# Moving the operands of a split-product stage to common byte residues in SBUF

## The reference

```python
x = x + tanh(g_xattn[0]) * L0_xattn(layernorm(x), ctx, ctx, W, b)       # single-head attention, 154 keys
x = x + tanh(g_ffn[0])   * L0_ffn(layernorm(x), Wg, Wu, Wd)             # 8 dense experts, all summed
x = x + tanh(g_xattn[1]) * L1_xattn(layernorm(x), ctx, mask, gamma, beta, Wq, Wkv, Wout)  # 8 heads
x = x + tanh(g_ffn[1])   * L1_ffn(layernorm(x), wg, W, b)               # top-1 routing, capacity 256
# L0_ffn, per expert: acc += (silu(x @ wg) * (x @ wu)) @ wd     wg, wu: 256 x 1024, wd: 1024 x 256
```

## The kernel before, in words

| operands of the split products | role | before: start byte | mod 2048 | mod 512 |
|---|---|---|---|---|
| xop_hi, xop_lo (blocks at steps of 2,048) | moving | 116,064 to 171,360 | 1376 | 352 |
| hid_hi, hid_lo (blocks at steps of 2,048) | moving | 65,792 to 96,512 | 256 | 256 |
| t_hi, t_lo | moving | 20,608 to 30,848 | 128 | 128 |
| w_hi, w_lo (blocks at steps of 512) | stationary | 173,408 to 205,664 | 4 values | 352 |
| wd_hi, wd_lo (blocks at steps of 512) | stationary | 187,744 to 209,760 | 4 values | 352 |
| wds_hi, wds_lo | stationary | 16,512 to 20,096 | 4 values | 128 |

## Time and profile before

### The profile page before, as it was taken

The page is one execution under the profiler, slowest core; times in us unless marked ns, Lnnn a source line. Parts: engine busy times, 40 slices in busy tenths (PEclk is TensorE's granted clock), DMA queues, the critical chain, the costliest instruction groups (busy, mean ns, idle before and its releaser), DMA issues.

```text
span 1258.8 us, 18431 instructions
## 1 busy us (share of the span) xinstructions
PE 1232.6 (98%) x6152; PEld 995.4 (79%) x6152; DVE 1054.3 (84%) x1775; ACT 729.2 (58%) x1509; POOL 880.5 (70%) x833
## 2 busy tenths in 40 slices
PE   7999999999999999999999999999999999999998
PEld 5778888888888888888888888888888887787775
DVE  5887889898899999999999999888999974667546
ACT  2455566656666666666666666666566545545543
POOL 3735688888887888888877888888888626443435
PEclk9999999999999999999999999999999999999999
DMA  4020200000110000000000000000100330000131
GB/s 137 26 92 1 94 26 26 26 26 26 41 36 26 26 26 26 26 26 26 26 26 26 26 26 26 26 26 31 42 29 1 117 118 1 18 26 10 35 98 63
DMA packets 42366, 48.28 MB, mean 38 GB/s; under 512 B 4239, under 2 KB 40143, under 8 KB 42015
## 3 DMA queue, kind: packets, MB, share of 16 engines
q1 hardware_dynamic: 38720, 43.07, 10.4%
q0 software_dynamic: 1440, 3.41, 0.8%
q10 hardware_dynamic: 2111, 0.63, 0.2%
HBM read 37.36 MB, written 10.29 MB: 38 GB/s over the span
## 4 chain that ended last, share of the span: by engine, by line
PE 91%; DVE 4%; ACT 3%; issue 1%; DMA 0%; POOLq 0%; ACTq 0%; POOL 0%; DVEq 0%
PE bank L1307 25%; PE bank L1308 25%; PE bank L1309 25%; ACT PC L1050 2%; PE bank L1545 2%; PE bank L1554 1%; PE bank L1269 1%; PE bank L1707 1%; PE bank L1724 1%; PE bank L1251 1%; DVE nmC L2101 1%; PE bank L1529 1%; PE bank L1213 1%; PE bank L1657 1%; PE bank L1479 1%
## 5 line engine op out<-in xcount | busy, mean ns | idle before, releaser
L1307 PE MATMUL bank<-xop_hi,w_hi 128*128 128x512 f32 x896 | 351.9, 393 | 1.7 <-ACT half_g L948 1.2
L1308 PE MATMUL bank<-xop_lo,w_hi 128*128 128x512 f32 x896 | 352.4, 393 | 0.0
L1309 PE MATMUL bank<-xop_hi,w_lo 128*128 128x512 f32 x896 | 351.4, 392 | 0.0
L1958 DVE TENSOR_TENSOR hid_lo<-hid,hid_hi 128x512 fp32r<-128x512 f32 x228 | 220.2, 979 | 14.1 <-ACT hid_hi L972 9.8
L1307 PEld LDWEIGHTS bank<-xop_hi,w_hi 128*128 128x128 f32 x896 | 168.9, 188 | 42.4 <-ACT half_g L948 1.5
L1308 PEld LDWEIGHTS bank<-xop_lo,w_hi 128*128 128x128 f32 x896 | 168.6, 188 | 38.2
L1309 PEld LDWEIGHTS bank<-xop_hi,w_lo 128*128 128x128 f32 x896 | 168.6, 188 | 37.7
L972 ACT CAST hid_hi<-hid 128x512 fp32r<-128x512 f32 x228 | 140.8, 622 | 57.9 <-DVE hid L1950 57.9
L956 ACT ACTIVATE s<-bank 128x512 f32<-128x512 f32 x128 | 78.3, 612 | 102.5 <-PE bank L1309 102.5
L1307 PE MATMUL bank<-hid_hi,wd_hi 128*128 128x512 f32 x344 | 136.2, 396 | 0.6 <-DVE hid_lo L1958 0.6
L1308 PE MATMUL bank<-hid_lo,wd_hi 128*128 128x512 f32 x344 | 136.2, 396 | 0.0
(11 more groups left out here) (273 smaller groups left out, 2615.1 us busy)
## 6 DMA issues: line engine op xcount, KB each, us to landing
raw_gu<-in_L_ffn_Wg_dram SPq DMA_DIRECT2D x32, 256.0 KB, 2.7
raw_gu<-in_L_ffn_Wu_dram SPq DMA_DIRECT2D x32, 256.0 KB, 3.1
raw_d<-in_L_ffn_Wd_dram SPq DMA_DIRECT2D x32, 256.0 KB, 3.7
slots<-empty_row SPq DMA_DIRECT2D x1, 2080.0 KB, 11.1
xr<-slots SPq DMA_DIRECT2D x8, 260.0 KB, 4.5
x_res<-in_x_dram SPq DMA_DIRECT2D x4, 512.0 KB, 5.3
x_mid<-x_res SPq DMA_DIRECT2D x1, 2048.0 KB, 9.2
x_res<-x_mid SPq DMA_DIRECT2D x4, 512.0 KB, 5.4
```

The lines of the kernel that those rows point to most:

```text
L1307: mm(ps, w, a, start=start, stop=False, skip_group_check=True)
L1308: mm(ps, w, a_low, start=False, stop=False, skip_group_check=True)
L1309: return mm(ps, w_low, a, start=False, stop=True, skip_group_check=True)
L1958: nc.vector.tensor_tensor(out=hid_lo[n % 2][h][:], in0=hid[h][:], in1=hid_hi[n % 2][h][:].bitcast(F32), op=ALU.subtract).then_inc(lo_ready ...
```

## The change

Arena gets a method that moves its next address up to a given residue modulo 2048. `ident`, `before` and the seven small `mv` tensors are now allocated ahead of `x_res`, which puts x_res at byte 17,760 (1376 modulo 2048; the gap that `align` itself adds there is 0 bytes). The `mv` tensors leave their old place, so `ones`, `A0`, `V0`, `ctxT` and their neighbours up to `stats` start 224 bytes later than before, and everything from `ve0` on stays where it was. `st` is aligned ahead of the hidden operands, which start 1,120 bytes later and now end at 99,680, the end of the room they overlay. `sx` starts where x_res does. No instruction, wait, loop or order is changed.

After it, hid_hi, hid_lo, t_hi and t_lo start at 1376 modulo 2048, and wds_hi and wds_lo at 352 modulo 512. The operands xop, w and wd, `acc`, and all tensors of stage C and E outside x_res, ones and mv, are where they were.

```diff
+ROW_BYTES = 2048
+OPERANDS_AT = 1376
 class Arena:
+    def align(self, residue):
+        self.at += (residue - self.at) % ROW_BYTES
+        assert self.at <= self.end, (self.at, self.end)
...
-        x_res = keep.take("x_res", [P, NT, D], F32)
+        LANES = NC + 3
+        LN_FRONT, LN_FRONT2, LN_ROUTE = range(NC, LANES)
         ident = keep.take("ident", [P, P], F32)
         before = keep.take("before", [P, P], F32)
+        mv = [keep.take(f"mv{i}", [P, CT, 2], F32) for i in range(LANES)]
+        keep.align(OPERANDS_AT)
+        x_at = keep.at
+        x_res = keep.take("x_res", [P, NT, D], F32)
...
-        LANES = NC + 3
-        LN_FRONT, LN_FRONT2, LN_ROUTE = range(NC, LANES)
         stats = [keep.take(f"stats{i}", [P, CT, 6], F32) for i in range(LANES)]
-        mv = [keep.take(f"mv{i}", [P, CT, 2], F32) for i in range(LANES)]
...
         hid_hi, hid_lo = [], []
+        st.align(OPERANDS_AT)
         for i in range(2):
             hid_hi.append({h: st.take(f"hid_hi{h}_{i}", [P, CH], F32R) for h in BLOCKS})
...
-        sx = Arena(nc, base, base + 4 * NT * D)
+        sx = Arena(nc, x_at, x_at + 4 * NT * D)
...
         acc = sb.take("acc", [P, KB, T], F32)
+        assert sb.at % ROW_BYTES == OPERANDS_AT
```

## The result

The kernel after takes 1241.12 us (median of 4 executions, 1240.56 to 1241.58), the kernel before 1257.16 (4 executions, 1256.47 to 1258.66): a ratio of 0.9869, 95% interval 0.9855 to 0.9883, 16.0 us less. Forecast were 1240.7 us and 16.5 less. In the code after, `three` stands at L1318 to L1320 (before L1307 to L1309).

The account below looks back on a forecast made before the run. TensorE's matmul issue was taken to bound the product stage; 16.0, 0.4 to 0.5 and 0.15 us sum to 16.5 us saved, taking the median from 1257.2 to 1240.7 us, chance 0.80, range 1238.5 to 1246.5.

Parts of the forecast that it names:

- the three terms: Product-stage gains: 16.0 us from 110 to 1010 us, 0.4 to 0.5 from 84 to 110, 0.15 from 1010 to 1019.9.
- The step that carried it: Product stage: every matmul gets the gate and up stream's 226.7 ns interval once its operands share that stream's residues.
- Costing a T triple together with the gate triple behind it: Triples on t or wds: six intervals at 6.6 ns extra, five times per couple of groups, 5.6 us over 28 couples.
- The prediction's worst case for the slack: VectorE's lost slack in the product stage gives back at worst 0.05 us in each of 28 couples, 1.5 us.
- The reading: Product stage: the floor of 226.7 ns needs both operands, and the next ones, at the same byte modulo 512.
- The 32 modulo 64: The prediction also gave the floor stream's shared start byte, 352 modulo 512, as 32 modulo 64.
- The slack at the bank sum: VectorE's bank sum ends 0.48 us before its matmul starts; some 0.18 us go, 0.3 remain, cost 0.
- that the engines' work stays the same: Product stage: other engines' work keeps its time, so VectorE has 27.08 of 29.24 us per couple of groups.
- Only part joins: Rival, chance 0.10: triples on t or wds keep their price, 5.6 us; gain 10.9, median 1246.3 us.
- Not the cause: Rival, chance 0.06: position in SBUF, not residues, explains the intervals, so nothing changes; 1257.2 us.
- Slower: Rival, chance 0.04: new residues put all 4,100 matmuls of the product stage at 233.3 ns, +10.3 us, 1267.5 us.
- The rule of the Trainium skill: Matmul spacing depends on columns alone (about 216 ns, or some 131 sustained), not start address; the change is worth nothing.

Follow-up runs that it names:

- experiment 8: Kernel before with only the hidden operands moved to 1376 modulo 2048, x_res, t and wds staying at 128: 1247.14 us, ratio 0.9916.
- experiment 9: Kernel after without the hidden operands' alignment (back at 256 modulo 2048), x_res, t and wds kept at their new places: 1252.16 us, ratio 0.9956 to before.
- experiment 11: Kernel after with hidden operands and wd at 128 modulo 256, the product stage's other operands at 96: 1255.21 us, ratio 0.9992 to before.
- experiment 6: Kernel after with hidden operands at 1120 modulo 2048, still 96 modulo 256: 1241.73 us, ratio 0.9875 to before.
- experiment 1: Kernel after with hidden operands at 288 modulo 2048 (32 modulo 64) instead of 1376: 1258.3 us, ratio 0.9993 to before.
- experiment 3: Kernel after with every tensor from x_res on 32 bytes higher, all operands at 128 modulo 256: 1240.85 us, ratio 0.9867 to before.
- experiment 4: Kernel after with weights w and wd 32 bytes higher, at 128 modulo 256, moving operands unmoved: 1264.96 us, ratio 1.0063 to before.
- experiment 10: Kernel after with weights w and wd 128 bytes higher, at 224 modulo 256: 1266.74 us, ratio 1.0071 to before.
- experiment 5: Kernel after with hidden operands at 864 modulo 2048, still 352 modulo 512: 1241.96 us, ratio 0.9881 to before.
- experiment 7: Kernel after with hidden operands at 1248 modulo 2048, 224 modulo 256: 1257.12 us, ratio 1.0 to before.
- experiment 12: Kernel after with stage C's query weights 96 bytes higher, at 352 modulo 512 like their moving operands: 1241.81 us, ratio 0.9866 to before.
- experiment 2: Kernel after with hidden operands 32 bytes lower, at 1344 modulo 2048: 1251.53 us, ratio 0.9953 to before.

## Why the prediction was right

**The bound and the sum.** The prediction took the product stage as paced by TensorE's starts and nothing else, and gave each of 3,900 matmuls between 110 and 1,010 us the interval of the earlier trace rows instead of 230.8: 16.0 us, and 0.5 around it. Counted at the same matmul in both traces, the three terms came out at 15.9 us (forecast 16.0), 0.46 (0.4 to 0.5) and 0.18 (0.15), and the stretch before 84 us, which was given nothing, at 0.3; the whole stage gave 16.8, the medians 16.0. The step that carried it, that the pace of the one stream at the floor is the pace of all once they share its residues, is right to 0.1 ns.

**Its parts.** The hidden operands were to give 10.9 us and t with wds 5.6; experiments 8 and 9 measured 0.84% and 0.44%, that is 10.6 and 5.5 us. Costing a T triple together with the gate triple behind it, six intervals each, was the right way to count: a triple that differs slows those behind it too. (The prediction's worst case for the slack, 0.05 us in 28 couples, is 1.4 us and not 1.5; nothing hangs on it.)

**The cause.** The reading was half right. "Both operands begin at the same byte modulo 512 and the next operands too": the second half is the one that decides, as experiments 8 and 11 show (a moving operand has to agree with the weights loaded beside it for the next matmul), and the modulus is 256 (experiment 6). The trace of before already held the exception: the interval from a gate triple into a T4 triple is at 226.7 ns, since wd agrees with xop, and only the next is at 236. The 32 modulo 64 that the prediction also named plays no part (1 and 3). That the forecast came out in spite of this is not insight but a safe choice: the change brings everything to one residue modulo 512, which meets every one of these conditions.

**What was to cost nothing.** The slack at the bank sum came out at 0.30 us where 0.3 was forecast, no wait took anything back, and TensorE is busy without a gap. One statement failed: that the engines' work stays the same. VectorE's hid_lo takes 73 ns longer and its t_lo 188 ns less, a couple of groups 27.32 us of VectorE instead of 27.08, so it is busy for 93.4% of the couple instead of the forecast 92.6. The new place of the hidden tensors isn't the reason: in experiments 4 and 10 they lie where they do after, and hid_lo takes 939 and 946 ns; in 3, 5 and 6 they lie elsewhere, and it takes 1046 to 1050. It is longest where TensorE's interval is shortest. It cost nothing as long as slack was left. x_res's first load takes 5.2 us per 512 KB (5.3 in the earlier trace rows), now that it begins at 32 modulo 64. Stage A is level at its end, so moving A0 and V0 neither cost nor gained anything.

**The rivals.** *Only part joins* falls by the trace of after: the T4 triple is at 226.7. *Not the cause*, with position in its stead, falls by experiment 4 (xop in place, at 233), by 6 and 7, and by 12. *Slower* was a real case, only not this change's: it asked for a stream in which every matmul stands at 233.3, 1267.5 us. Experiments 4 and 10 are such streams, at 232.9 and 1264.96 and 1266.74 us. What the rival had wrong is which relation brings it about: agreement of the residues doesn't raise the interval, disagreement does.

**The rule of the Trainium skill.** "TensorE: Matmul & The Clock Gate", section "Back-to-back issue gap", by which the spacing depends on the columns alone, would have had the change worth nothing. By that rule experiments 3 and 4 would be equal; they are 226.8 and 232.9 ns, and 24 us apart.

## What to carry to other kernels

Where TensorE is busy without a gap, look at the distances between the starts of equal matmuls: if they have more than one value, something besides the number of matmuls is being paid for. Here it was where in SBUF the operands begin, and one alignment of arenas took 1.3% off the kernel without changing an instruction. Align the moving and the stationary operands of a stream, and those of any stream woven into it, to one byte modulo 256 (96 and 128 were tried and do equally well); a moving operand has to agree with the weights of the next matmul, not only with its own. Bringing only some of them there gives only their share. Then look at what the faster engine has left of slack elsewhere, here 0.30 of 0.48 us.

## What the runs showed of the hardware

- For one-pass float32 matmuls of 128 x 512, each with its 128 x 128 weight load, the interval is 226.7 ns (544 cycles at 2.4 GHz) when the moving operand of each matmul and the weights of the next start at the same byte modulo 256, and 233 ns on average (560 cycles) when they differ throughout. With one mismatch nearly throughout, 32 and 128 bytes cost the same (experiments 4 and 10); with hid triples off among others that agree, the mean is 229.4, 229.7, 230.1 and 230.2 ns for 32, 96, 64 and 128 bytes (2, 9, 1 and 7).
- Behind a stretch at the floor, the first pair that differs takes its own interval to 232 to 236 ns, and up to ten intervals behind it, in which all agree, lie off the floor too (before, 1, 2, 7, 8, 9 and 11). Why isn't shown.
- VectorE's subtraction into `hid_lo` takes from 939 to 1050 ns on average (110 to 1,000 us) for one shape: 939 and 946 where TensorE's interval is 233 ns (4 and 10), 974 to 993 where it is 229 to 231 (before, 1, 2, 7, 9 and 11), 1019 where it is 228.3 (8), 1046 to 1050 where it is 226.7 (after, 3, 5, 6 and 12). It goes with the pace of the stage and not with the place of its tensors. Its cause is open.
- Starts that differ by less than 32 bytes, other shapes and other formats weren't tried.
